# Second expert mixture: outputs copied aside before they are added, and the block's steps in another order

## The chip, the cores and the metric

The kernel runs on one core of one Trainium2 chip. The metric is device time in microseconds (us): 885.04 us before the change, the median of three runs (881.98 to 886.37). A profiled execution gives the trace; its span is 889.0 us.

## The reference

Two transformer layers over 2048 tokens of width 256 (2 batches of 1024), with a context of 154 rows per batch. Each layer is a cross attention and then a mixture of experts; both have a residual, and a layer norm ahead of them. The change lies in the mixture of the second layer:

```
logits = x @ Wg.T                      # 8 experts
top_v, top_i = top_k(logits, 2)        # two experts per token
gates = softmax(top_v)
# each expert takes at most 640 tokens
h = einsum('ecd,edf->ecf', exp_batches, W1)   # width 2 x 512
inp, gate = split(h, 2)
h = gelu(inp, exact) * gate
exp_out = einsum('eci,eid->ecd', h, W2)       # back to 256
out = segment_sum(gate_of_token * exp_out, token)
```

## The kernel before, in words

Both mixtures work in the same way, with the same functions and a layer object `l` (`l.n` is 0 or 1, `l.r` its prefix for semaphores, "r0" or "r1"). The normalised rows of the tokens are scattered by expert into a DRAM tensor `rows`, each row as two float16 parts (high and low) and four numbers at its end: the token, the second gate, the gain and the first expert. A table on the chip says at which block each expert begins. A block is 256 rows; where the last block of an expert holds at most 128 rows, TensorE computes only 128 of them. The second mixture has 19 blocks: experts of 3, 3, 1, 3, 1, 3, 3 and 2 blocks, of which 13 are whole and 6 are half blocks, each the last of its expert.

All products are made of float16 parts: high times high, high times low, low times high. In the second mixture the hidden width is 512, four chunks of 128 or two pairs of chunks (`pairs` is 2). One block g goes through the engines like this:

- ScalarE's queue loads the rows of a block into `x_raw` (L1253, `load`, two blocks ahead). TensorE turns them (L933, `turn_block`, one block ahead, after the gate and up products of block g), and VectorE copies the turned rows from PSUM into `xbT` (L1783) and works out each row's token and gate into `carried` (L1786 to L1790); this is `turned`. `x_raw` may be loaded again when `carried` is written.
- TensorE makes gate and up products (L685, output to `ps`) of pair 0 and pair 1, 48 matmuls. ScalarE applies Gelu (L1267), VectorE multiplies with the up product (L1804, into `h32`), ScalarE casts to float16 (L1271, `h_hi`), VectorE takes the difference (L1809, `h_lo`).
- TensorE makes the down products (L685, 24 matmuls in a whole block, 12 in a half one): in a first pass all high chunks, in a second all low chunks. It waits for the output of block g-1 to have left PSUM (semaphore `_y`).
- ScalarE scales the outputs into `yb` (L1280, two instructions). It waits for the down products and until the addition of block g-1 has landed (semaphore `_added`), since there is one `yb`.
- GpSimd (POOL) copies the token numbers of the block into `row_to` (L571), waits for `yb`, and issues two indirect DMAs that add 128 rows each to the output in DRAM (L575). It waits until both have landed (`_stored`), signals `_added` (L580), and only then goes on to the next block. Between experts it also loads the next two entries of the table (L567, L568).

The weights of an expert come in three chunks of 128x1024 float32. In the first block of each of the experts 0 to 5 the chunks of the expert two further on are split: ScalarE casts the high part (L1129, `high_part`), VectorE subtracts the low part (L1405). `l.beside` and `l.low_beside` say after which step of the block which chunk comes. Each engine works through its own program in order; nothing but these semaphores sets the order between engines. POOL's program is the loop `add_results`, called by `rest_of_experts`.

Of the kernel before, what the change touches and what calls it, by code (L numbers as in the profile page):

```python
# [22 lines left out]
P = 128  # L23
# [5 lines left out]
E = 8  # L29
# [42 lines left out]
def two_layers(nc, a, out):  # L72
    with ExitStack() as ctx:
# [183 lines left out]
        blk_passed = sb("blk_passed", [P, AHEAD, E], BF16)  # L257
        row_to = sb("row_to", [P, 2], I32)
        slot_s = sb("slot_s", [P, NT, TOP], I32)
        cnt = sb("cnt", [P, E])  # L260
# [231 lines left out]
        def _(pool):  # L492
# [71 lines left out]
            def add_results(l, e):  # L564
# [4 lines left out]
                with pool.Fori(first, end) as g:  # L569
# [10 lines left out]
                    pool.sem_inc(S(r + "_added"), 1)  # L580

            def scale_phi():

# [15 lines left out]
            def rest_of_experts(l):  # L599
                pool.wait_ge(S(l.r + "_kept"), 16 * NG)  # L600
                pool.wait_ge(S(l.r + "_table"), 1)
                with pool.Fori(0, E - 1) as e:
                    add_results(l, e)
                add_results(l, E - 1)

# [77 lines left out]
        def _(pe):  # L683
# [240 lines left out]
            def experts(l):  # L924
# [12 lines left out]
                def one_block(g, wh, wl, width):  # L937
# [15 lines left out]
                    turn_block(g + 1)  # L953
                    pe.wait_ge(S(r + "_y"), g + 1)
                    for c in range(l.hc):
                        if c % 2 == 0:
# [152 lines left out]
        def _(act):  # L1109
# [133 lines left out]
            def experts(l):  # L1243
# [11 lines left out]
                def one_block(g, coming=None):  # L1255

                    def split(step):
                        if coming:
                            for n in l.beside[step]:
                                high_part(l, *coming, n)  # L1260

                    for j in range(pairs + 1):
                        n = g * pairs + j
# [11 lines left out]
                    load(g + 2)  # L1275
                    split(pairs)
                    act.wait_ge(S(r + "_down"), g + 2)
                    wait_counted(act, S(r + "_added"), g + 1)
                    for hf in range(2):
# [22 lines left out]
                act.wait_ge(S(r + "_xbT_ps"), 2)  # L1302
                act.wait_ge(S(r + "_carried"), 1)
                load(1)
# [72 lines left out]
        def _(dve):  # L1377
# [397 lines left out]
            def experts(l):  # L1775
# [5 lines left out]
                def turned(g):  # L1781
# [8 lines left out]
                    dve.tensor_tensor(own[:, :, 0], share[:, :], raw[:, :, SECOND], ALU.add).then_inc(S(r + "_carried"), 1)  # L1790

                raw = x_raw[:, :, :].bitcast(F32)
                def low_part(e, slot, n):
                    low_part_of(l, e, slot, n)

                def one_block(g, coming=None):

                    for j in range(pairs + 1):
                        n = g * pairs + j
# [36 lines left out]
                else:  # L1836
                    coming_low_parts(1)
                turned(0)
                with dve.Fori(0, E // l.slots - 1) as pr:
# [136 lines left out]
```

## Time and profile before

| | |
|---|---|
| median of 3 runs | 885.04 us (881.98 to 886.37) |
| span of the profiled execution | 889.0 us |
| busy in the span: PE, DVE, ACT, POOL | 700.3, 547.8, 403.1, 302.8 us |
| second mixture, first to last block on PE | 711 to 872 us of the span |
| PE busy from 711 to 880 us | 144.60 of 169.00 us |

The span is the time from the first to the last instruction of the profiled execution, which was a little longer than the three timed runs. Times in the rows are microseconds from the start of the span. In a row of the timeline the bracket gives how long the engine had been idle before it and what ended that.

### The profile page before, as it was taken

What the parts mean: (1) busy time and instruction counts of PE and PEld (TensorE: products, weight loads), DVE (VectorE), ACT (ScalarE), POOL (GpSimd) and SP (SyncE); (2) the same over time, 40 slices, a digit from 0 to 9 for tenths busy, and PEclk for the clock granted to TensorE, in tenths of its full rate; (3) what the DMA queues carried; (4) which work ended last, traced back from release to release, by engine and by line L of the source; (5) the groups of instructions that cost most, each with busy time, mean ns of one, the idle gap of its engine ahead of it and who ended that gap; (6) DMA issues with size and microseconds to landing.
All of it is one profiled execution on the core that took longest, in us unless ns stands there. A gap on an engine that the chain in (4) does not pass through costs nothing.

```text
span 889.0 us, 19049 instructions
## 1 busy us (share of the span) xinstructions
PE 700.3 (79%) x6278; PEld 550.1 (62%) x6278; DVE 547.8 (62%) x1322; ACT 403.1 (45%) x720; POOL 302.8 (34%) x306
## 2 busy tenths in 40 slices
PE   5476796989564799999999899996862098898981
PEld 4232454555354688888897798895531087777771
DVE  7768576887836545647556656547696446566441
ACT  1135466576513434646545555442552044546331
POOL 7505301416337422222121131232167414334342
PEclk9689799989776799999999999997875599999996
DMA  4562300601524542536344643425022555464332
GB/s 140 118 141 51 59 2 24 180 24 49 153 81 151 185 129 36 165 51 171 78 126 98 170 112 101 107 39 179 25 101 95 174 170 131 115 147 114 63 55 40
DMA packets 68418, 92.24 MB, mean 104 GB/s; under 512 B 14442, under 2 KB 54435, under 8 KB 68348
## 3 DMA queue, kind: packets, MB, share of 16 engines
q1 hardware_dynamic: 41788, 63.37, 24.1%
q0 software_dynamic: 14592, 16.24, 10.6%
q10 hardware_dynamic: 11968, 11.72, 5.3%
q8 instruction: 42, 0.69, 0.3%
q14 instruction: 28, 0.23, 0.1%
HBM read 64.21 MB, written 29.87 MB: 106 GB/s over the span
## 4 chain that ended last, share of the span: by engine, by line
PE 48%; DVE 18%; issue 11%; ACT 9%; POOL 5%; DMA 5%; ACTq 2%; another core or an unknown queue 1%; DVEq 0%; POOLq 0%; SPq 0%
PE ps L685 45%; POOL rows L631 3%; DVE probs L1726 3%; DVE mx L1591 2%; DMA out_x<-keys,row_to 2%; DVE keys L1804 2%; DMA probs<-rows 2%; ACT probs L1189 1%; ACT probs L1271 1%; ACT expo L1186 1%; DVE keys L1783 1%; ACT probs L1267 1%; PE ps L933 1%; DVE stats L1383 1%; ACTq L1252 1%
## 5 line engine op out<-in xcount | busy, mean ns | idle before, releaser
L1804 DVE TENSOR_TENSOR keys<-probs,ps 128x512 f32<-128x512 f32 x122 | 82.8, 687 | 177.3 <-ACT probs L1267 86.3
L685 PE MATMUL ps<-keys,slot 128*128 128x256 f16 (+1 forms) x1440 | 146.5, 263 | 5.4 <-DVE keys L1783 2.7
L685 PE MATMUL ps<-keys,probs 128*128 128x256 f16 (+1 forms) x1488 | 139.5, 255 | 5.1 <-DVE probs L1405 3.7
L685 PEld LDWEIGHTS ps<-keys,slot 128*128 128x128 f16 x1440 | 127.8, 99 | 22.8 <-issue 5.4
L685 PEld LDWEIGHTS ps<-keys,probs 128*128 128x128 f16 x1488 | 124.2, 98 | 19.0 <-issue 7.2
L575 POOL DMA_INDIRECT attended<-keys,row_to x42 | 67.2, 1601 | 166.0 <-ACT keys L1280 142.2
L1267 ACT ACTIVATE probs<-ps 128x512 f32<-128x512 f32 x122 | 71.4, 598 | 65.9 <-PE ps L685 63.7
L1280 ACT ACTIVATE keys<-ps,carried 128x256 f32<-128x256 f32 x80 | 33.5, 470 | 117.9 <-POOLq L580 41.6
L1809 DVE TENSOR_TENSOR probs<-keys,probs 128x512 f16<-128x512 f32 x122 | 83.3, 688 | 3.6 <-ACT probs L1271 1.9
L1271 ACT CAST probs<-keys 128x512 f16<-128x512 f32 x122 | 74.8, 614 | 22.0 <-DVE keys L1804 21.9
L1726 DVE TENSOR_TENSOR probs<-expo,probs 128x512 f16<-128x512 f32 x80 | 61.1, 775 | 34.1 <-ACT probs L1189 28.2
L685 PE MATMUL ps<-slot,probs 128*128 128x256 f16 x636 | 74.8, 273 | 3.7 <-ACT probs L1271 3.0
L685 PE MATMUL ps<-probs 128*128 128x256 f16 x612 | 72.4, 273 | 4.8 <-ACT probs L1271 4.4
L575 POOL DMA_INDIRECT out_x<-keys,row_to x38 | 58.8, 1548 | 45.6 <-ACT keys L1280 36.6
L1186 ACT ACTIVATE expo<-ps 128x512 f32<-128x512 f32 x80 | 48.2, 602 | 52.8 <-PE ps L685 46.9
L685 PEld LDWEIGHTS ps<-slot,probs 128*128 128x128 f16 x636 | 60.0, 98 | 14.4 <-ACT probs L1271 4.2
L685 PEld LDWEIGHTS ps<-probs 128*128 128x128 f16 x612 | 57.5, 98 | 15.8 <-ACT probs L1271 4.5
L571 POOL COPY row_to<-carried 128x2 int32 x40 | 10.1, 252 | 139.0 <-issue 45.5
L933 PE MATMUL ps<-identh,probs 128*128 128x128 f16 x336 | 26.5, 224 | 36.5 <-DMA probs<-rows 36.5
L685 PE MATMUL ps<-penalties,identb 128*128 128x462 bf16 x96 | 34.8, 363 | 22.2 <-DVE queries L1569 9.4
L1189 ACT CAST probs<-expo 128x512 f16<-128x512 f32 x80 | 49.0, 619 | 0.0
L1405 DVE TENSOR_TENSOR probs<-inbox,probs 128x1024 f16<-128x1024 f32 x36 | 43.6, 1221 | 6.1 <-ACT probs L1129 6.0
(285 smaller groups left out, 1145.7 us busy)
## 6 DMA issues: line engine op xcount, KB each, us to landing
inbox<-in_W SPq DMA_DIRECT2D x24, 512.0 KB, 3.9
probs<-rows ACTq DMA_DIRECT2D x44, 260.0 KB
inbox<-in_wg SPq DMA_DIRECT2D x16, 512.0 KB, 5.2
inbox<-in_wu SPq DMA_DIRECT2D x16, 512.0 KB, 3.7
inbox<-in_wd SPq DMA_DIRECT2D x16, 512.0 KB, 4.2
rows<-zeros SPq DMA_DIRECT2D x16, 260.0 KB
x<-in_x SPq DMA_DIRECT2D x4, 512.0 KB, 6.1
q_out<-queries SPq DMA_DIRECT2D x8, 256.0 KB, 2.1
```

Source lines behind the costliest of these rows:

```text
L575: pool.indirect_dma_start(out=l.sums, out_offset=bass.IndirectOffsetOnAxis(ap=row_to[:, hf:hf + 1], axis=0), in_=yb[:, hf, :], in_offset=N ...
L685: return pe.matmul(o, l, r, start=start, stop=stop, **kw)
L933: last = pe.transpose(psh[:, 6, part * BLK + hf * P:part * BLK + (hf + 1) * P], x_raw[:, hf, part * P:(part + 1) * P], identh[:, :])
L1186: act.activation(e_ring[:, u % 4, :], ps[:, 4 + u % 2, :], ACT.Exp, scale=float(DK) ** -0.5).then_inc(S("a0_exp"), 1)
L1189: act.copy(p_hi[:, u - 1, :], e_ring[:, (u - 1) % 4, :]).then_inc(S("a0_phi"), 1)
L1267: act.activation(s_act[:, j % 2, :], ps[:, 2 * (j % 2), :], l.act).then_inc(S(r + "_s"), 1)
L1271: act.copy(h_hi[:, 2 * j - 2:2 * j, :].rearrange("p c t -> p (c t)"), h32[:, (j - 1) % 2, :]).then_inc(S(r + "_hh"), 1)
L1280: ins = act.activation(yb[:, hf, :], ps[:, 4 + hf, 0:D], ACT.Identity, scale=carried[:, bass.ds(g, 1), hf, 0:1].rearrange("p b d -> p (b d)"))
L1405: dve.tensor_tensor(w[:, 1, at:at + CH], stage[:, n % STAGES, :], w[:, 0, at:at + CH], ALU.subtract).then_inc(S(f"w_ready{l.n}"), 1)
L1726: dve.tensor_tensor(p_lo[:, u, :], e_ring[:, u % 4, :], p_hi[:, u, :], ALU.subtract).then_inc(S("a0_plo"), 1)
L1804: dve.tensor_tensor(h32[:, j % 2, :], s_act[:, j % 2, :], ps[:, 2 * (j % 2) + 1, :], ALU.mult).then_inc(S(r + "_h32"), 1)
L1809: dve.tensor_tensor(h_lo[:, 2 * j - 2:2 * j, :].rearrange("p c t -> p (c t)"), h32[:, (j - 1) % 2, :], h_hi[:, 2 * j - 2:2 * j, :].rearran ...
```

## The change

All of it is for the second mixture (`l.n` is 1); the first keeps its code.

- GpSimd copies `yb` into a new tensor `y_sent` (128x512 float32) after it has waited for `yb`, and the two indirect DMAs read from `y_sent`. A new semaphore `_taken` says that the copy is made. ScalarE's outputs wait for `_taken` of block g-1 and no longer for `_added`.
- TensorE's down products go pair by pair: high and low chunks of pair 0, then of pair 1, 24 matmuls as before.
- `turned` is cut in two. `turned_rows` copies the turned rows into `xbT` and the four numbers of each row into a new small tensor `tail_now` (128x8), which frees `x_raw` (semaphore `_raw_free`); it stands ahead of the difference of the last pair. `own_shares` works out `carried` from `tail_now`, after that difference.
- ScalarE's order in a block is Gelu, cast, Gelu, cast, where it was Gelu, Gelu, cast, cast. VectorE's is product, difference, product, (turned rows), difference.
- Of the three weight chunks ScalarE casts the first after the load and ahead of the outputs, the two others after the outputs; VectorE takes all three differences at the end of the block.

The core of the diff:

```
+        y_sent, _ = part(keys, 0, [P, 2, D])
-            l.beside = (([0], [1], [2], [3, 4], [5]), ([0], [1, 2], []))[n]
-            l.low_beside = (([0], [1], [2], [3], [4, 5]), ([0], [], [1, 2]))[n]
+            l.beside = (([0], [1], [2], [3, 4], [5]), ([], [0], [1, 2]))[n]
+            l.low_beside = (([0], [1], [2], [3], [4, 5]), ([], [], [0, 1, 2]))[n]
+            def copy_and_add_results(l, e):
...
+                with pool.Fori(first, end) as g:
+                    wait_counted(pool, S(r + "_carried"), g + 1)
+                    pool.tensor_copy(row_to[:, :], carried[:, bass.ds(g, 1), :, 1].bitcast(I32).rearrange("p b h -> p (b h)")).then_inc(S(r + "_to"), 1)
+                    wait_counted(pool, S(r + "_to"), g + 1)
+                    wait_counted(pool, S(r + "_y"), g + 2)
+                    pool.tensor_copy(y_sent[:, :, :], yb[:, :, :]).then_inc(S(r + "_taken"), 1)
+                    wait_counted(pool, S(r + "_taken"), g + 2)
+                    for hf in range(2):
+                        pool.indirect_dma_start(
+                            out=l.sums, out_offset=bass.IndirectOffsetOnAxis(ap=row_to[:, hf:hf + 1], axis=0),
+                            in_=y_sent[:, hf, :], in_offset=None, bounds_check=N - 1, oob_is_err=False,
+                            compute_op=ALU.add).then_inc(S(r + "_stored"), 16)
+                    pool.wait_ge(S(r + "_stored"), g * 32 + 32)
+                    pool.sem_inc(S(r + "_added"), 1)
...
+                def outputs_by_pairs(g, wh, wl, width):
+                    for j in range(pairs):
+                        pe.wait_ge(S(r + "_hh"), g * pairs + j + 1)
...
+                                mm(o, h_hi[:, c, tk], wh[:, at:at + D], c == 0, False)
+                                mm(o, h_hi[:, c, tk], wl[:, at:at + D], False, False)
+                        pe.wait_ge(S(r + "_h"), g * pairs + j + 3)
...
+                                last = mm(o, h_lo[:, c, tk], wh[:, at:at + D], False, c == l.hc - 1)
...
+                        act.wait_ge(S(r + "_xbT_ps"), g + 3)
+                        act.wait_ge(S(r + "_raw_free"), g + 2)
+                        load(g + 2)
+                        split(pairs - 1)
+                        results(g)
+                        split(pairs)
...
+                def results(g):
                     act.wait_ge(S(r + "_down"), g + 2)
-                    wait_counted(act, S(r + "_added"), g + 1)
+                    wait_counted(act, S(r + ("_taken" if l.n else "_added")), g + 1)
...
+                def turned_rows(g):
+                    dve.wait_ge(S(r + "_xbT_ps"), g + 2)
+                    dve.tensor_copy(xbT[:, :, :, :].rearrange("p a b c -> p (a b c)"), psh[:, 6, :]).then_inc(S(r + "_xbT"), 1)
+                    wait_counted(dve, S(r + "_share"), g + 1)
+                    dve.tensor_copy(tail_now[:, :, :], raw[:, :, TOKEN:TOKEN + 4].bitcast(I32)).then_inc(S(r + "_raw_free"), 1)
```

On POOL, the loop over the blocks of the last expert of the second mixture; `yb` and `y_sent` both lie in the arena `keys`. Before:

```order
L571 ISA [waits r1_carried]
L571 COPY row_to<-carried 128x2
L322 REGISTER_ALU [waits r1_to]
L575 DMA out_x<-keys,row_to 2048x256 [waits r1_y]
L575 DMA out_x<-keys,row_to 2048x256
L579 ISA
L569 REGISTER_ALU [waits r1_stored]
L569 COMPARE_AND_BRANCH
```

The same loop after the change:

```order
L591 ISA [waits r1_carried]
L591 COPY row_to<-carried 128x2
L324 REGISTER_ALU [waits r1_to]
L594 COPY keys<-keys 128x512 [waits r1_y]
L597 DMA out_x<-keys,row_to 2048x256 [waits r1_taken]
L597 DMA out_x<-keys,row_to 2048x256
L601 ISA
L589 REGISTER_ALU [waits r1_stored]
L589 COMPARE_AND_BRANCH
```

One copy stands between the wait for `_y` and the first DMA, and the DMA now waits for that copy; the wait for `_stored` at the end of the turn is where it was.

On ACT, the end of the first block of an expert, where the weights of a later expert are cast (`probs<-inbox`) and the outputs are written (`keys<-ps,carried`). Before:

```order
L1129 CAST probs<-inbox 128x1024 [waits staged_0]
L1270 REGISTER_ALU
L1271 CAST probs<-keys 128x512 [waits r1_h32]
L1129 CAST probs<-inbox 128x1024 [waits staged_1]
L1129 CAST probs<-inbox 128x1024 [waits staged_2]
...
L1253 DMA probs<-rows 128x2x260
L322 REGISTER_ALU [waits r1_down]
L1280 ISA [waits r1_added]
L1280 ACTIVATE keys<-ps,carried 128x256
L1280 ISA
L1280 ACTIVATE keys<-ps,carried 128x256
```

After the change:

```order
L1317 CAST probs<-keys 128x512 [waits r1_h32]
...
L1301 DMA probs<-rows 128x2x260
L1177 CAST probs<-inbox 128x1024 [waits staged_0]
L324 REGISTER_ALU [waits r1_down]
L1348 ISA [waits r1_taken]
L1348 ACTIVATE keys<-ps,carried 128x256
L1348 ISA
L1348 ACTIVATE keys<-ps,carried 128x256
L1177 CAST probs<-inbox 128x1024 [waits staged_1]
L1177 CAST probs<-inbox 128x1024 [waits staged_2]
```

The load of rows is issued ahead of all three weight casts; one cast stands ahead of the outputs and two behind them, and the outputs wait for `_taken`.

## Rows read from the trace of the kernel before

**Rows 1.** The page: the span, and the last difference of a pair on DVE.
```profile
span 889.0 us, 19049 instructions
...
L1809 DVE TENSOR_TENSOR probs<-keys,probs 128x512 f16<-128x512 f32 x122 | 83.3, 688 | 3.6 <-ACT probs L1271 1.9
```

**Rows 2.** Busy time by engine in the second mixture: start:end, length, busy (instructions).
```profile
711.00:880.00 169.00, 144.60 (x1448) 121.07 (x1448) 89.19 (x173) 76.88 (x133) 63.98 (x57) 0.97 0.50 110
```

**Rows 3.** Waits between 705 and 889 us: who for whom, total, times, longest.
```profile
ACT keys L1280 <- POOLq L580: 41.6, 11, 4.4
```

**Rows 4.** PE's timeline: start, length, line, idle before. Two whole blocks around a half.
```profile
746.99 5.41 PE L685 MATMUL ps<-keys,slot 128*128 128x256 f16 x48
...
755.59 2.84 PE L685 MATMUL ps<-keys,slot 128*128 128x128 f16 x48
...
762.13 5.41 PE L685 MATMUL ps<-keys,probs 128*128 128x256 f16 x48 [0.28 <-DVE keys L1783]
```

**Rows 5.** POOL's timeline: first and last addition, and first and last handover within an expert.
```profile
725.76 1.60 POOL L575 DMA_INDIRECT out_x<-keys,row_to  x1 [13.88 <-ACT keys L1280]
...
732.20 0.19 POOL L571 COPY row_to<-carried 128x2 int32 x1 [2.96 <-DMA out_x<-keys,row_to]
...
875.11 0.19 POOL L571 COPY row_to<-carried 128x2 int32 x1 [2.96 <-DMA out_x<-keys,row_to]
876.43 1.55 POOL L575 DMA_INDIRECT out_x<-keys,row_to  x1 [1.14 <-ACT keys L1280]
878.29 1.54 POOL L575 DMA_INDIRECT out_x<-keys,row_to  x1 [0.30 <-issue]
```

**Rows 6.** POOL's timeline: the seven handovers at an expert's begin, with one's DMAs.
```profile
748.18 0.38 POOL L571 COPY row_to<-carried 128x2 int32 x1 [3.30 <-DVE carried L1790]
...
774.57 0.19 POOL L571 COPY row_to<-carried 128x2 int32 x1 [4.74 <-issue]
775.80 1.55 POOL L575 DMA_INDIRECT out_x<-keys,row_to  x1 [1.04 <-issue]
777.66 1.54 POOL L575 DMA_INDIRECT out_x<-keys,row_to  x1 [0.30 <-issue]
782.94 0.21 POOL L571 COPY row_to<-carried 128x2 int32 x1 [3.74 <-DVE carried L1790]
...
807.93 0.54 POOL L571 COPY row_to<-carried 128x2 int32 x1 [3.28 <-DVE carried L1790]
...
818.22 1.24 POOL L571 COPY row_to<-carried 128x2 int32 x1 [4.32 <-issue]
...
843.80 0.19 POOL L571 COPY row_to<-carried 128x2 int32 x1 [3.89 <-issue]
...
867.14 0.19 POOL L571 COPY row_to<-carried 128x2 int32 x1 [3.02 <-issue]
```

**Rows 7.** Costliest groups on POOL, by shape: a cast of 128 and a memset of 512.
```profile
L511 POOL MEMSET slot<- 128x512 f32 x1 | 0.5, 515 | 0.0
...
L502 POOL CAST identb<-ident 128x128 bf16<-128x128 f32 x1 | 0.3, 291 | 0.1
```

**Rows 8.** One line of POOL, float32 in, 256 wide: shortest/median/longest in ns.
```profile
L650 POOL CAST penalties<-xln x8: 397/398/498, 197.6 to 270.8; 128x256 f16<-128x256 f32 x8
```

**Rows 9.** ACT's timeline: the end of the first block.
```profile
719.66 1.99 ACT L1129 CAST probs<-inbox 128x1024 f16<-128x1024 f32 x2
723.36 0.38 ACTq L1253 DMA_DIRECT2D probs<-rows  x1
724.03 0.84 ACT L1280 ACTIVATE keys<-ps,carried 128x256 f32<-128x256 f32 x2 [2.38 <-issue]
```

**Rows 10.** DVE's timeline: low parts of weights at the end of a block.
```profile
817.06 2.35 DVE L1405 TENSOR_TENSOR probs<-inbox,probs 128x1024 f16<-128x1024 f32 x2
```

**Rows 11.** PE's timeline: the last down products of the first block.
```profile
721.50 0.61 PE L685 MATMUL ps<-slot,probs 128*128 128x256 f16 x4 [0.20 <-DVE probs L1809]
```

**Rows 12.** One line of POOL, 256 wide, once beside a DVE difference: shortest/median/longest.
```profile
L527 POOL CAST heads<-heads x3: 399/688/1488, 88.3 to 92.9; 128x256 bf16<-128x256 f32 x3
```

More of the change, by code:

```diff
@@ L258, in two_layers @@
         row_to = sb("row_to", [P, 2], I32)
+        tail_now = sb("tail_now", [P, 2, 4], I32)
         slot_s = sb("slot_s", [P, NT, TOP], I32)
@@ L580, in add_results @@
                     pool.sem_inc(S(r + "_added"), 1)
+            def copy_and_add_results(l, e):
+                tb, r = table[l.n], l.r
+                first = pool.value_load(tb[0:1, bass.ds(e, 1)], min_val=0, max_val=MAXBLK - 1)
+                end = pool.value_load(tb[0:1, bass.ds(e + 1, 1)], min_val=1, max_val=MAXBLK)
+                with pool.Fori(first, end) as g:
[12 more added lines that the diff above has]
+                    pool.sem_inc(S(r + "_added"), 1)
             def scale_phi():
@@ L601, in rest_of_experts @@
                 pool.wait_ge(S(l.r + "_table"), 1)
+                add = add_results if l.n == 0 else copy_and_add_results
+                if l.n:
+                    pool.sem_inc(S(l.r + "_taken"), 1)
                 with pool.Fori(0, E - 1) as e:
-                    add_results(l, e)
-                add_results(l, E - 1)
+                    add(l, e)
+                add(l, E - 1)
             def power(c, t0, n):
@@ L1260, in split @@
                                 high_part(l, *coming, n)
+                    if l.n:
+                        for j in range(pairs):
+                            n = g * pairs + j
+                            act.wait_ge(S(r + "_h32"), n + 1)
+                            act.wait_ge(S(r + "_gu_ps"), n * 2 + 1)
+                            act.activation(s_act[:, j % 2, :], ps[:, 2 * (j % 2), :], l.act).then_inc(S(r + "_s"), 1)
+                            act.wait_ge(S(r + "_h32"), n + 3)
+                            act.copy(h_hi[:, 2 * j:2 * j + 2, :].rearrange("p c t -> p (c t)"), h32[:, j % 2, :]).then_inc(S(r + "_hh"), 1)
+                            if j < pairs - 1:
+                                split(j)
+                        act.wait_ge(S(r + "_xbT_ps"), g + 3)
[4 more added lines that the diff above has]
+                        split(pairs)
+                        return
                     for j in range(pairs + 1):
@@ L1796, in one_block @@
                 def one_block(g, coming=None):
+                    if l.n:
+                        for j in range(pairs):
+                            n = g * pairs + j
+                            dve.wait_ge(S(r + "_s"), n + 1)
+                            dve.wait_ge(S(r + "_gu_ps"), n * 2 + 2)
+                            dve.wait_ge(S(r + "_h"), n + 1)
+                            dve.tensor_tensor(h32[:, j % 2, :], s_act[:, j % 2, :], ps[:, 2 * (j % 2) + 1, :], ALU.mult).then_inc(S(r + "_h32"), 1)
+                            if j == 0:
+                                dve.wait_ge(S(r + "_down"), g + 1)
+                            if j == pairs - 1:
+                                turned_rows(g + 1)
+                            dve.wait_ge(S(r + "_hh"), n + 1)
+                            dve.tensor_tensor(h_lo[:, 2 * j:2 * j + 2, :].rearrange("p c t -> p (c t)"), h32[:, j % 2, :],
+                                              h_hi[:, 2 * j:2 * j + 2, :].rearrange("p c t -> p (c t)"), ALU.subtract).then_inc(S(r + "_h"), 1)
+                        own_shares(g + 1)
+                        if coming:
+                            for c in l.low_beside[pairs]:
+                                low_part(*coming, c)
+                        return
                     for j in range(pairs + 1):
```

32 lines of the change are left out of this document (30 added, 2 removed).

## The prediction

> **What bounds the kernel now.** I read the page first, then the busy times by stretch, then the waits and the timelines of the second mixture, engine by engine. The change touches only that mixture, some 169 us of a span of 889.0 us, in which PE is busy for 144.60 us [rows 1, 2]. So PE has little idle time to give back there, and the question is who makes it idle. The waits name POOL: ScalarE's outputs waited 41.6 us in 11 cases for the signal that an addition has landed [rows 3]. PE's timeline shows what that does: a whole block with nothing in its way takes 8.60 us (746.99 to 755.59), a half block 6.54 us (755.59 to 762.13), although its matmuls are only half as many [rows 4]. All 13 whole and 6 half blocks at these paces would be 151.0 us.
>
> Next to this stands POOL's own loop, which decides my forecast. Its 19 turns run from the first addition at 725.76 to the last at 876.43 us, 18 intervals in 150.67 us, 8.37 us each [rows 5]. A turn has parts that it can't avoid: from the end of the second DMA issue to the next `row_to` copy (the landing and the loop) 2.94 us on average over the 11 handovers within an expert (the first and the last are 2.96) [rows 5]; the copy itself 0.19; 1.04 from the copy to the DMA where nothing is waited for; two issues of 1.55 and 1.54 with 0.30 between them, 3.39 [rows 6]. That is 7.56 us. At the seven handovers to a new expert, where POOL also loads table entries, the idle time ahead of the copy is 3.30, 4.74, 3.74, 3.28, 4.32, 3.89 and 3.02 us, 3.76 on average, so the turn has 8.38 us; and four of these copies took 0.38, 0.21, 0.54 and 1.24 us, together 1.6 us more than 0.19 each [rows 6]. The sum of what POOL can't avoid is 11 x 7.56 + 7 x 8.38 + 1.6 = 143.4 us. POOL therefore has only 150.67 - 143.4 = 7.3 us to spare in the whole mixture. Before, it is nearly as much the bound as PE.
>
> **The change part by part.** *The copy on POOL.* Each turn gets a copy of 128x512 float32 and one more counted wait, behind the landing of the block before and ahead of its own DMAs, so all of it lies on POOL's loop. No row shows this copy. From below: a memset of that shape, which reads nothing, took 0.515 us [rows 7]. The casts read float32 at 291 ns for 128 elements [rows 7] and 398 ns for 256 [rows 8], 0.84 ns per further element; carried on to 512 that is 0.61 us, and I take this. The added wait: from the end of a `row_to` copy to the DMA there were 1.04 us with two waits already met [rows 6], and from the end of ScalarE's output (724.03 + 0.84) to the DMA at 725.76 us 0.89 us with one [rows 5, 9]; so a wait costs about 0.15. A turn grows by 0.76 us, 18 of them by 13.7 us.
>
> *The copy beside VectorE.* At 818.22 us a `row_to` copy took 1.24 us, and it ended at 819.46, just when a pair of weight differences that began at 817.06 and lasted 2.35 us had ended at 819.41 [rows 6, 10]. A POOL copy that meets such a difference waits for its end. The differences of a block take 2 x 0.688 us [rows 1], and in six of 19 blocks three weight differences of some 1.2 us come on top, 1.16 us per block: 2.5 us in 8.4, a chance of 0.3, and half a difference to wait (0.46 us), 0.14 us per turn or 2.5 us in all. The Trainium skill, page "SBUF — State Buffer", section "Who interferes with whom", states this as a lock: a VectorE instruction with two SBUF inputs and a GpSimd instruction that reads SBUF block each other, the second to come waiting until the first has finished. By this rule the 2.5 us belong in the sum, and the rows agree; without it the forecast would be 2.5 us lower. The lock would also hold VectorE back by up to a copy's length, which costs nothing as long as PE isn't the bound.
>
> *ScalarE waits for the copy.* The wait that goes (41.6 us) doesn't free POOL: its DMAs are issued, and their landing waited for, in the same order and number. What it gives is one block more of lead for PE. PE uses it up: its first 18 blocks at the paces of rows 4 need 144.5 us, POOL's 18 turns now need 143.4 + 13.7 + 2.5 = 159.6. Whatever lead PE gets, it ends by waiting for `_y` again, that is for POOL's copy. The stall moves from ScalarE's wait for `_added` to ScalarE's and PE's waits for `_taken` and `_y`.
>
> *The first output.* Before, ScalarE cast two weight chunks until 721.65 us, issued a load at 723.36 and wrote the first output at 724.03, although PE's down products had ended at 722.11 [rows 9, 11]. With the load earlier and two casts behind the output it may begin at about 722.3, 1.7 us earlier; the first copy takes 0.76 of it back. The first addition starts 1.0 us earlier.
>
> *The rest.* Down products by pairs are the same 24 matmuls with other waits; Gelu and cast in turn make the chain of a half block longer by about a cast and a difference (1.3 us at most), and the earlier output gives some of it back; the tail copy (128x8) adds one short instruction to VectorE per block; the earlier free `x_raw` starts loads earlier. The cast that now stands ahead of the outputs waits for its staged chunk, and the output, PE's next down products and POOL's copy are queued behind it; the two casts behind the outputs delay the next block's first Gelu, and all three differences the next product. I cost all of this at nothing either way: the 15 us by which PE is ahead of POOL over the mixture cover it. If that cover is gone it would be up to 1.3 us in each half block, 8 us, or the same gained from the loads.
>
> **The sum.** 13.7 + 2.5 - 7.3 (POOL's spare time, used up) - 1.0 = +7.9 us. What follows the last issue (878.29 + 1.54 to 889.0, 9.2 us) stays [rows 1, 5]. So the profiled span goes from 889.0 to about 897 us; it is 4 us over the median of the runs shown, and the same difference on that median, 885.04, gives 892.9 us, 0.9% slower.
>
> **The rivals.** *PE sets the end (faster).* If POOL's turns shrink by themselves, for instance because landings and table loads at an expert's begin (3.02 to 4.74 us) are as short as those within (2.94), that takes 7 x 0.8 + 1.6 = 7 us off its loop; with the copy at its lower end (9.3 us) POOL would need 146 us and PE's 151.0 us would decide, from about 161 us now (its first to last block, 711 to 872 us): at most 10 us less; I take 7, 878 us. For it speaks the wait of 41.6 us; against it, that the cases with 4.74 and 3.89 us waited for nothing shown, thus are POOL's own time. It decides from the point where a turn with its copy is below PE's 7.9 us on average. Chance 0.12.
>
> *No change.* The copy costs its lower bound, 0.515 us, and the wait nothing: 9.3 - 7.3 - 1.2 = +0.8, 886 us. For it speaks that the price of 0.61 us is carried on from casts of half the size; against it, that a memset doesn't read. Chance 0.22.
>
> *The copy is slow.* A cast of 256 elements on POOL took 1.488 us where others took 399 ns [rows 12]; a copy of 512 hit like that takes 1.70 us, a turn 1.85 more, 33 us in all, or +25 us; if half of the copies are hit, +16 us, 901 us. For it speaks that the weight differences now come together, close to the time of the outputs. Chance 0.08.
>
> **How the numbers follow.** The forecast, POOL's loop longer by its copy, has 0.58; its own range is 888 to 899 us (a turn longer by 0.5 to 1.1 us, the rest of the sum as it stands). 0.5% of 885.04 is 4.4 us, about what a measurement of this kernel tells from no change. Faster (below 880.6): the first rival, 0.12. Same (to 889.5): the second and a small part of the forecast's own range, 0.25. Slower: 0.63. The range of 884 to 903 us leaves out the first rival and the worst of the third.
>
> **What would show it.** Right: POOL's additions 8.4 to 9.3 us apart from the third block on, nearly all with "issue" ahead of them and no wait for ScalarE; the new copy at 0.6 us, longer where VectorE subtracts; PE idle ahead of its down products, waiting for `keys` outputs; last addition at about 884 us of the span. Wrong: POOL waiting for ScalarE before most copies, or additions 8.0 us apart or closer; PE's blocks at 8.6 and 6 us without idle time to the end.

## The result, and the profile after

The changed kernel takes 904.95 us (median of 4 runs, 900.27 to 908.31) beside 884.08 us of the kernel before on the same chip: ratio 1.0225, 95% interval 1.0195 to 1.0256. The forecast was 892.9 us with a range of 884 to 903: slower, as forecast, but by 21 us where 8 were worked out.

On the page of the changed kernel, the span, the group of POOL's additions (busy, mean ns of one, idle before) and the weights' loads by SP (median us from issue to landing):

```profile
span 902.0 us, 19115 instructions
...
L597 POOL DMA_INDIRECT out_x<-keys,row_to x38 | 62.6, 1648 | 22.5 <-POOL keys L594 16.8
...
inbox<-in_W SPq DMA_DIRECT2D x24, 512.0 KB, 5.3
```

The mean issue is 1648 ns, where it was 1.55 and 1.54 us [rows 6], and no idle time of POOL's DMAs is put down mainly to ScalarE any more.

Busy time by engine in the second mixture (start:end, length, then PE, PE weight loads, DVE, ACT, POOL, granted clock, DMA share, GB/s):

```profile
704.60:890.00 185.40, 150.21 (x1448) 124.19 (x1448) 93.49 (x192) 77.49 (x133) 77.47 (x75) 0.92 0.44 100
```

Against [rows 2] the stretch is 16 us longer with the same 1448 matmuls; PE stands idle for 35 us where it did for 24. PE's busy time grew by 5.6 us; the granted clock, a mean between its two levels of 1.2 and 2.4 GHz, is 0.92 of the upper one, where it was 0.97, in a stretch in which PE stands idle longer. The mixture now begins at 704.65 us, in the profile before at 711.12; the two profiled runs differ by 6 us before the change's code begins, so that the spans differ by 13 and the medians by 21. I therefore compare the time from the first to the last addition.

POOL's timeline, the first two DMAs, a turn with nothing in its way, and the last two (start, length, idle before):

```profile
717.63 1.79 POOL L597 DMA_INDIRECT out_x<-keys,row_to  x1 [0.89 <-POOL keys L594]
719.72 1.58 POOL L597 DMA_INDIRECT out_x<-keys,row_to  x1 [0.30 <-issue]
...
797.72 0.19 POOL L591 COPY row_to<-carried 128x2 int32 x1 [2.86 <-DMA out_x<-keys,row_to]
798.24 0.61 POOL L594 COPY keys<-keys 128x512 f32<-128x512 f32 x1 [0.33 <-POOL row_to L591]
799.73 1.56 POOL L597 DMA_INDIRECT out_x<-keys,row_to  x1 [0.88 <-POOL keys L594]
801.59 1.54 POOL L597 DMA_INDIRECT out_x<-keys,row_to  x1 [0.30 <-issue]
...
889.42 1.56 POOL L597 DMA_INDIRECT out_x<-keys,row_to  x1 [0.88 <-POOL keys L594]
891.29 1.54 POOL L597 DMA_INDIRECT out_x<-keys,row_to  x1 [0.30 <-issue]
```

From 717.63 to 889.42 are 171.8 us in 18 turns, where [rows 5] have 150.7: 21.1 us more, about the whole of the loss. In a free turn `row_to` ends at 797.91 and the DMA begins at 799.73: 1.82 us (0.33 + 0.61 + 0.88), where it was 1.04. All 18 turns show this 1.82 within 0.03 us, so POOL waits for no output after the first.

But the turns at a new expert look otherwise. POOL's timeline there:

```profile
775.08 0.44 POOL L591 COPY row_to<-carried 128x2 int32 x1 [5.57 <-issue]
...
777.36 2.37 POOL L597 DMA_INDIRECT out_x<-keys,row_to  x1 [0.88 <-POOL keys L594]
780.04 2.48 POOL L597 DMA_INDIRECT out_x<-keys,row_to  x1 [0.31 <-issue]
789.44 0.18 POOL L591 COPY row_to<-carried 128x2 int32 x1 [6.92 <-issue]
...
818.37 1.04 POOL L591 COPY row_to<-carried 128x2 int32 x1 [6.53 <-issue]
```

DVE's weight differences at that time, SP's weight loads there, and two pieces of the chain of waits (start, length, what):

```profile
777.07 1.23 DVE L1473 TENSOR_TENSOR slot<-inbox,slot 128x1024 f16<-128x1024 f32 x1 [1.07 <-ACT slot L1177]
778.74 2.36 DVE L1473 TENSOR_TENSOR slot<-inbox,slot 128x1024 f16<-128x1024 f32 x2 [0.45 <-ACT slot L1177]
...
818.14 1.23 DVE L1473 TENSOR_TENSOR probs<-inbox,probs 128x1024 f16<-128x1024 f32 x1 [1.07 <-ACT probs L1177]
```

```profile
778.47 3.13 SPq L425 DMA_DIRECT2D inbox<-in_W  x3
```

```profile
780.04 7.26 DMA out_x<-keys,row_to
...
801.59 3.78 DMA out_x<-keys,row_to
```

The handovers of 5.57, 6.92 and 6.53 us answer to 4.74, 3.74 and 4.32 in [rows 6]. Two things happen at 777 to 790 us. The two issues take 2.37 and 2.48 us instead of 1.55, and beside them VectorE subtracts weights from 777.07 to 778.30 and from 778.74 to 781.10. And the second addition lands 7.26 us after its issue began, against 3.78 us for one with no loads beside it; three weight chunks of 512 KB were issued from 778.47 on within 3.13 us.

POOL's 18 turns, cut into their parts (sums from POOL's timeline of each run; us). The columns: the 11 handovers within an expert, the 7 at a new expert, the 36 issues, the `row_to` copies, and the time from `row_to` to the first DMA; with the 0.30 between two issues 18 times, they make the time from the first to the last addition.

| | first to last | within | new expert | issues | `row_to` | to the DMA |
|---|---|---|---|---|---|---|
| before | 150.7 | 32.3 | 26.3 | 55.7 | 5.0 | 25.9 |
| after | 171.8 | 35.4 | 33.2 | 59.5 | 5.4 | 32.9 |
| more | 21.1 | 3.1 | 6.9 | 3.8 | 0.4 | 7.0 |

The last column is the forecast's own term: 18 x 0.78 = 14.0 us of copy and wait, less the 7 us that POOL had waited. The other 14 us were not in it.

### The profile page after: what moved, and what is told of

Read it like the earlier page. It is cut to its first block, busy times and chain, and to the rows that moved or that the text cites. A ratio compares the mean times of both kernels' runs of the same rounds, so it can differ in the third digit from the quotient of the medians.

```text
span 902.0 us, 19115 instructions
## 1 busy us (share of the span) xinstructions
PE 706.6 (78%) x6266; PEld 556.6 (62%) x6278; DVE 552.0 (61%) x1342; ACT 403.7 (45%) x720; POOL 318.9 (35%) x325
## 4 chain that ended last, share of the span: by engine, by line
PE 43%; DVE 16%; issue 13%; DMA 10%; POOL 7%; ACT 7%; POOLq 2%; ACTq 1%; DVEq 0%; SPq 0%
PE ps L710 40%; DMA out_x<-keys,row_to 7%; POOL rows L656 3%; DVE probs L1794 3%; DVE mx L1659 2%; ACT probs L1237 1%; POOL keys L594 1%; ACT expo L1234 1%; PE ps L958 1%; POOL out_x L597 1%; DVE stats L1451 1%; DVE keys L1907 1%; DMA probs<-rows 1%; POOL row_to L591 1%; DVE probs L1912 1%
## 5 line engine op out<-in xcount | busy, mean ns | idle before, releaser
L710 PE MATMUL ps<-keys,slot 128*128 128x256 f16 (+1 forms) x1440 | 149.2, 266 | 4.8 <-DVE keys L1907 2.5
L710 PE MATMUL ps<-keys,probs 128*128 128x256 f16 (+1 forms) x1488 | 141.9, 257 | 4.7 <-DVE probs L1473 3.8
L1794 DVE TENSOR_TENSOR probs<-expo,probs 128x512 f16<-128x512 f32 x80 | 61.0, 774 | 33.4 <-ACT probs L1237 33.2
L1332 ACT ACTIVATE probs<-ps 128x512 f32<-128x512 f32 x84 | 50.0, 597 | 53.1 <-PE ps L710 52.7
L597 POOL DMA_INDIRECT out_x<-keys,row_to x38 | 62.6, 1648 | 22.5 <-POOL keys L594 16.8
L1912 DVE TENSOR_TENSOR probs<-keys,probs 128x512 f16<-128x512 f32 x84 | 57.6, 685 | 1.5 <-ACT probs L1336 0.3
L1336 ACT CAST probs<-keys 128x512 f16<-128x512 f32 x84 | 51.5, 613 | 12.2 <-DVE keys L1907 12.1
```

Of the source, the lines that this page charges most:

```text
L597: pool.indirect_dma_start(out=l.sums, out_offset=bass.IndirectOffsetOnAxis(ap=row_to[:, hf:hf + 1], axis=0), in_=y_sent[:, hf, :], in_offs ...
L710: return pe.matmul(o, l, r, start=start, stop=stop, **kw)
L1332: act.activation(s_act[:, j % 2, :], ps[:, 2 * (j % 2), :], l.act).then_inc(S(r + "_s"), 1)
L1336: act.copy(h_hi[:, 2 * j - 2:2 * j, :].rearrange("p c t -> p (c t)"), h32[:, (j - 1) % 2, :]).then_inc(S(r + "_hh"), 1)
L1794: dve.tensor_tensor(p_lo[:, u, :], e_ring[:, u % 4, :], p_hi[:, u, :], ALU.subtract).then_inc(S("a0_plo"), 1)
L1912: dve.tensor_tensor(h_lo[:, 2 * j - 2:2 * j, :].rearrange("p c t -> p (c t)"), h32[:, (j - 1) % 2, :], h_hi[:, 2 * j - 2:2 * j, :].rearran ...
```

## The experiments

The question is where the other 14 us come from. They may come from the moved weight casts and the loads that follow them; from the copy, which makes POOL late; or from the new order of products, Gelu and casts. And what lengthens issues and landings may be the weight loads in the DMA engines, or VectorE's subtractions beside POOL, or both. Every kernel was timed in 3 or 5 rounds beside the kernel before. The letters in the expectations are explained where they stand, D and L under the small loads; the text below goes by what each theory says. The times are medians of several runs, the time from the first to the last addition comes from one profiled execution of each kernel, so that the two can differ by some microseconds.

**The copy alone** (kernel before, with POOL's copy and ScalarE's wait for `_taken`; all else as before).

```
-                    wait_counted(act, S(r + "_added"), g + 1)
+                    wait_counted(act, S(r + ("_taken" if l.n else "_added")), g + 1)
...
+                    pool.tensor_copy(y_sent[:, :, :], yb[:, :, :]).then_inc(S(r + "_taken"), 1)
+                    wait_counted(pool, S(r + "_taken"), g + 2)
```

> The kernel before with nothing but the copy to y_sent, the additions from it, and ScalarE's outputs waiting for the copy. Theory A (the copy lengthens POOL's loop by 0.78 us a turn, and the additions land late only because the weight casts were moved, which makes three weight loads start together beside them): 18 x 0.78 = 14.0, less the 7.3 us that POOL had to spare, +7 us, 891 us, landings as before. Theory B (a loop that is always late meets the weight loads wherever the casts stand): about +18 to +20 us, 903 us, with landings of 6 to 8 us as in the changed kernel.

Measured 901.06 us, ratio 1.0179 (1.0149 to 1.0208); first to last addition 164.4 us, 14 more than before. Of the two times expected, 891 us (the copy costs its own term and the moved casts the rest) and 903 us, the second is the nearer one: the moved casts are not needed for a loss of about 16 us (1.8%). POOL's timeline at one of its two late handovers, and SP's loads there:

```profile
766.34 2.35 POOL L596 DMA_INDIRECT out_x<-keys,row_to  x1 [0.88 <-POOL keys L593]
768.99 1.54 POOL L596 DMA_INDIRECT out_x<-keys,row_to  x1 [0.30 <-issue]
777.05 1.04 POOL L590 COPY row_to<-carried 128x2 int32 x1 [6.52 <-issue]
```

```profile
764.55 4.32 SPq L424 DMA_DIRECT2D inbox<-in_W  x3
```

The pair is issued in the middle of the loads. In the kernel before the loads of this place are issued between two pairs; SP's timeline there:

```profile
770.76 4.32 SPq L423 DMA_DIRECT2D inbox<-in_W  x3
```

The last of the three is issued by 775.08 us, and the next pair at 775.80 [rows 6]. So with the casts at their old place, too, the copy costs more than its own 7 us.

**The change without the copy** (ScalarE waits for `_added` again).

```
-                add = add_results if l.n == 0 else copy_and_add_results
+                add = add_results
...
-                    wait_counted(act, S(r + ("_taken" if l.n else "_added")), g + 1)
+                    wait_counted(act, S(r + "_added"), g + 1)
```

> The changed kernel without the copy: additions from yb, ScalarE's outputs wait for the landing again; all else (pairs, early turned rows, moved casts) stays. Theory A: the 13.7 us of longer landings and issues stay in part, less POOL's 7.3 us to spare, about +4 to +7 us, 890 us. Theory B: without the copy the loop isn't late, about the time before, 884 us. Theory C (ScalarE's new order Gelu, cast, Gelu, cast makes PE's blocks longer, and that is the loss): close to the changed kernel, 900 us or more, with PE idle inside its down products and POOL waiting for ScalarE.

896.49 us, 1.0113 (1.0081 to 1.0144): between the 890 us expected of the moved casts and the 900 us expected of the new order. **The casts and differences back** in the changed kernel:

```
-            l.beside = (([0], [1], [2], [3, 4], [5]), ([], [0], [1, 2]))[n]
-            l.low_beside = (([0], [1], [2], [3], [4, 5]), ([], [], [0, 1, 2]))[n]
+            l.beside = (([0], [1], [2], [3, 4], [5]), ([0], [1, 2], []))[n]
+            l.low_beside = (([0], [1], [2], [3], [4, 5]), ([0], [], [1, 2]))[n]
...
-                            if j < pairs - 1:
-                                split(j)
+                            split(j)
...
+                            if coming:
+                                for c in l.low_beside[j]:
+                                    low_part(*coming, c)
```

> The changed kernel with the weight casts and differences where they stood before (first chunk after the first pair's cast and difference, the two others after the second pair's cast and at the end of the block); the copy and all else stay. Theory A: the longer landings and issues (13.7 us) go, 905 - 13 = 892 us, additions about 8.8 us apart. Theory B: no gain, 902 to 905 us. Theory C: no gain, 902 to 905 us.

897.63 us, 1.0149 (1.0119 to 1.0178): again between the times expected, 892 us and 902 or more. **The casts moved, alone**, in the kernel before (the same two lines the other way, and the casts behind the outputs):

```
-                    split(pairs)
+                    split(pairs if l.n == 0 else pairs - 1)
...
+                    if l.n:
+                        split(pairs)
```

> The kernel before with nothing but the weight casts and differences moved as in the change (first cast ahead of the outputs, two behind them, three differences at the block's end). Theory A: some of the 13.7 us of longer landings and issues appear, less the 7.3 us to spare, +4 to +7 us, 890 us. Theory B and theory C: no change, 884 us.

899.5 us, 1.0162 (1.0132 to 1.0192), more than any theory gave it (890 us at most). First to last addition of the three: 165.7, 165.1 and 166.6 us. So between the additions the copy alone costs 14 us and the moved casts alone 16, and together they cost 21 (by the times about 16, 14 and 20): they don't add. None of the theories A, B and C covers these four runs. In the change without the copy a turn has no copy in it, and POOL's timeline still has a handover of 7.45 us, at a place where SP issues three loads:

```profile
746.45 2.01 POOL L577 DMA_INDIRECT out_x<-keys,row_to  x1 [0.30 <-issue]
755.91 0.19 POOL L573 COPY row_to<-carried 128x2 int32 x1 [7.45 <-DMA out_x<-keys,row_to]
757.23 1.55 POOL L577 DMA_INDIRECT out_x<-keys,row_to  x1 [1.14 <-ACT keys L1346]
```

```profile
744.41 3.13 SPq L425 DMA_DIRECT2D inbox<-in_W  x3
```

**The order alone** (the change without the copy and with the casts back: pairs, Gelu and cast in turn, rows turned early).

> The changed kernel without the copy and with the weight casts where they stood before: what is left is the pairs one by one, Gelu and cast in turn, and the rows turned ahead of the last difference. Theory D: POOL is late where it was before, so no landing grows, 884 us, within 4 us. If the order by itself moves additions onto the loads: 890 us or more.

884.52 us (10 runs), 0.9995 (0.9977 to 1.0013); 151.3 us. The order costs and gains nothing within 2 us, so the new order of Gelu and casts is not the loss.

**Small loads** (of the weights of the last six experts of the second mixture only 64 of 1024 columns of a chunk are loaded; the rest of each weight is missing), in the changed kernel and in the one before.

```
+                few = CH // 16 if l.n and not isinstance(e, int) else CH
-                sp.dma_start(stage[:, n % STAGES, :], w[:, col:col + CH]).then_inc(S(f"staged_{n}"), 16)
+                sp.dma_start(stage[:, n % STAGES, 0:few], w[:, col:col + few]).then_inc(S(f"staged_{n}"), 16)
```

> The changed kernel, but the weight loads of the second mixture's experts 2 to 7 bring only 64 of 1024 columns of each chunk (so the outputs of these experts are not the reference's); number, order and waits of all instructions stay. Theory D (an addition that is under way when three weight loads start lands only when these have landed, because they share the DMA engines): handovers fall to 2.9 us within an expert and about 3.5 at a new one, the first to the last addition take about 159 us and the time is 892 us. Theory L (VectorE's weight differences, with two inputs in SBUF, hold up POOL's making of descriptors and its table loads; the loads have no part): no change, 903 to 906 us, landings of 6 to 8 us stay.

> The kernel before with the same small weight loads (outputs of experts 2 to 7 of the second mixture are not the reference's). Theory D: little is held up by the loads before the change, since additions start behind two of three loads: 0 to 5 us less, 881 to 885 us. If it gains more than 8 us, the loads cost the kernel before too, by another way than the additions.

The changed kernel falls to 895.0 us (1.0115, 1.0082 to 1.0147), 164.5 us; the kernel before stays at 883.57 (0.9992, 0.9972 to 1.0012). So full loads cost the kernel before nothing and the changed one some 10 us, 7.3 of them between the additions. Of the times expected for the changed kernel, 892 us if additions wait for the loads is nearer than 903 if the loads have no part, but it isn't reached. In POOL's timeline the handovers shrink, the issues do not:

```profile
800.50 2.07 POOL L598 DMA_INDIRECT out_x<-keys,row_to  x1 [0.88 <-POOL keys L595]
802.87 2.54 POOL L598 DMA_INDIRECT out_x<-keys,row_to  x1 [0.31 <-issue]
808.69 0.21 POOL L592 COPY row_to<-carried 128x2 int32 x1 [3.28 <-issue]
```

**Small differences** (full loads; VectorE subtracts only 32 of the 1024 columns for these experts).

```
-                dve.tensor_tensor(w[:, 1, at:at + CH], stage[:, n % STAGES, :], w[:, 0, at:at + CH], ALU.subtract).then_inc(S(f"w_ready{l.n}"), 1)
+                few = 32 if l.n and not (isinstance(e, int) and e < 2) else CH
+                dve.tensor_tensor(w[:, 1, at:at + few], stage[:, n % STAGES, 0:few], w[:, 0, at:at + few], ALU.subtract).then_inc(S(f"w_ready{l.n}"), 1)
```

> The changed kernel, but VectorE's weight differences of the experts 2 to 7 in the second mixture take 32 of 1024 columns (their low parts are not the reference's); the loads are whole. Theory D: landings of 6 to 8 us stay beside the loads, 900 to 905 us; only the DMA issues that had grown (1.55 to 2.4 us) fall back, 3 to 4 us at most. Theory L: landings fall to 3.8 us, 892 us.

906.04 us, 1.0232 (1.0196 to 1.0267), 174.0 us, at the upper end of the 900 to 905 us expected if landings beside the loads stay long. Now the issues are short and the landings long; POOL's timeline at the same place:

```profile
776.63 1.56 POOL L597 DMA_INDIRECT out_x<-keys,row_to  x1 [0.88 <-POOL keys L594]
778.50 1.54 POOL L597 DMA_INDIRECT out_x<-keys,row_to  x1 [0.30 <-issue]
787.87 0.19 POOL L591 COPY row_to<-carried 128x2 int32 x1 [7.82 <-issue]
```

In the chain of waits the second of these additions lands 7.22 us after its issue began, although the issue itself is as short as ever (from the start of the issue, then SP's loads there):

```profile
778.50 7.22 DMA out_x<-keys,row_to
```

```profile
775.37 4.04 SPq L425 DMA_DIRECT2D inbox<-in_W  x3
```

The two runs separate the two mechanisms. The differences make the issues long: 59.5 us in the changed kernel, 55.9 with small differences. The loads make the landings long: all 18 handovers take 68.6 us in the changed kernel and 60.6 with small loads. Neither is the whole. Beside full loads the differences cost no time of their own: when they go, the landings take as much.

**The copy alone with small loads.**

> The kernel before with GpSimd's copy and the outputs that wait for the copy alone; and of the weights of the last six experts of the second mixture only 64 of 1024 columns of each chunk are loaded (the rest is what lay there before). With full loads the copy alone gave 901 us, 17 us over the kernel before; a copy and its wait of 0.76 us in 18 turns less 7.3 us to spare explain 7 us of them. If the other 10 us come from additions that meet the weight loads: handovers at a new expert back to about 27 us in seven (30.75 with full loads), within an expert about 32 in eleven, first to last addition 156 to 159 us, about 892 us. If the copy alone costs more by itself (GpSimd and VectorE at one time, or the copy's own turn): first to last addition 162 us or more, 898 us or more.

896.11 us, 1.0135 (1.0112 to 1.0158), 163.1 us: between the two cases and nearer to the second one, against the theory that the loads are all that the copy meets. The handovers at a new expert fell to 25.1 us, but the issues grew to 60.9. Then **both small**, in the changed kernel (e14 in the second expectation) and with the copy alone:

> The changed kernel; of the weights of the last six experts of the second mixture only 64 of 1024 columns of each chunk are loaded and only 32 subtracted on VectorE. If loads and differences together make up what lies above the copy's own term: issues 55.7 us (3.10 a pair), handovers at a new expert about 26 us and within an expert about 32, between the additions 33, first to last addition 156 to 159 us, 889 to 892 us. If something else than these two makes GpSimd's turns longer: 162 us or more, 895 us or more.

> The kernel before with the copy alone, and weights' loads and differences small as in e14. If loads and differences together make up what lies above the copy's own term: issues 55.7 us, first to last addition 156 to 158 us, 890 to 892 us (before 884, copy and wait 14 us less the 7 that were to spare). If the copy costs more by itself: still 896 us.

890.32 us (10 runs; 1.0063, 1.0042 to 1.0084) and 890.88 us (7 runs; 1.0067, 1.0040 to 1.0094); first to last addition 158.3 and 157.3 us, 7.6 and 6.6 more than before. The same place in POOL's timeline of the changed kernel with both small:

```profile
775.83 1.56 POOL L598 DMA_INDIRECT out_x<-keys,row_to  x1 [0.88 <-POOL keys L595]
777.70 1.54 POOL L598 DMA_INDIRECT out_x<-keys,row_to  x1 [0.31 <-issue]
782.98 0.18 POOL L592 COPY row_to<-carried 128x2 int32 x1 [3.74 <-issue]
```

Its second addition lands after 3.13 us, with an issue as long as in the run with small differences alone, where it took 7.22:

```profile
777.70 3.13 DMA out_x<-keys,row_to
```

This closes the account of the sums: with small loads and differences the change costs 7.6 us between the additions and about 6 us in the time, which is the copy's own term of 7 us; the copy costs nothing further by itself. The two are not additive (171.8 us with both, 164.5 without the loads, 174.0 without the differences, 158.3 without either): the differences cost nothing beside full loads and 6.2 us beside small ones. A likely reason is that an addition that no longer meets the one comes at another moment and meets the other; it was not followed from place to place.

**One loop for the additions** (POOL adds all 19 blocks in one loop, without table loads between experts), in the kernel before, in the order alone, in the changed kernel, and in the changed kernel with the casts back.

```
-                first = pool.value_load(tb[0:1, bass.ds(e, 1)], min_val=0, max_val=MAXBLK - 1)
-                end = pool.value_load(tb[0:1, bass.ds(e + 1, 1)], min_val=1, max_val=MAXBLK)
+                first = 0 if e is None else pool.value_load(tb[0:1, bass.ds(e, 1)], min_val=0, max_val=MAXBLK - 1)
+                end = pool.value_load(tb[0:1, 8:9] if e is None else tb[0:1, bass.ds(e + 1, 1)], min_val=1, max_val=MAXBLK)
```

> The kernel before, but GpSimd adds all 19 blocks of the second mixture in one loop instead of one loop for each expert, so that no table entries are loaded between experts. If GpSimd's turns with their table loads set the pace of the kernel before nearly as much as the products do (7.3 us to spare, worked out from the handovers): the seven handovers at a new expert fall from 26.3 us to about 20.6 (2.94 each), first to last addition 146 to 149 us, 879 to 882 us, 0.2 to 0.5% faster. If the products alone set the pace: the handovers fall, ScalarE's waits for the addition fall too, and the time stays at 884 us within 1 us.

> The order of the change (products by pairs, Gelu and cast in turn, rows turned early) without the copy and with the weight casts where they were before, which gave 884.5 us and a first to last addition of 151.3 us; now GpSimd adds all 19 blocks of the second mixture in one loop, no table loads between experts. If GpSimd bounds this order: handovers at a new expert from 27.6 to about 21 us, first to last addition 145 to 148 us, 878 to 881 us. If the products bound it: 884 us within 1 us.

> The changed kernel, but GpSimd adds all 19 blocks of the second mixture in one loop, without table loads between experts. In the kernel before this took 10.8 us off the handovers and nothing off the time. If GpSimd's turns bound the changed kernel in all its blocks: what goes from the seven handovers (10 us, from 33 to about 23) comes off the time, 893 to 898 us. If the loads, met at another moment, or the products hold it: 901 us or more.

> The changed kernel with the weight casts and differences where they were before (897.6 us, first to last addition 165.1 us), and GpSimd's additions in one loop without table loads between experts. If GpSimd's turns are the bound: the handovers at a new expert from 31 to about 20 us, first to last addition about 154 us, 885 to 888 us; with the shorter turns the products may come to bound the end, and it can't get under about 880 us. If the loads decide: 893 us or more.

Kernel before: 884.46 us (12 runs; 1.0008, 0.9994 to 1.0023). Its handovers at a new expert fell from 26.3 to 15.5 us, and the time from `row_to` to the DMA rose from 25.9 to 37.3: what POOL saved it waited for outputs. Two rows of its timeline:

```profile
742.47 0.18 POOL L571 COPY row_to<-carried 128x2 int32 x1 [1.81 <-DMA out_x<-keys,row_to]
746.35 1.54 POOL L575 DMA_INDIRECT out_x<-keys,row_to  x1 [3.69 <-ACT keys L1283]
```

The order alone: 882.36 us (12 runs; 0.9988, 0.9969 to 1.0006), not to be told from the kernel before. The changed kernel: 897.84 us (1.0148, 1.0111 to 1.0186), 7 us less than 904.95 and within the 893 to 898 expected of POOL as the bound; its handovers at a new expert fell by 7.3 us, the time between the additions by 5.0. There POOL's own time is the bound, in the kernel before it is not. With the casts back: 893.9 us (1.0098, 1.0066 to 1.0131), where 885 to 888 were expected of POOL as the bound and 893 or more if the loads decide: the handovers at a new expert fell by 7.6 us, but the issues grew by 1.6, the handovers within an expert by 1.8 and `row_to` and what follows it up to the DMA by 1.4, so that only 2.8 us were left. That the additions came at other moments is the likely reason. No version here beats the kernel before by more than its interval.

## Why the prediction was right and where it was wrong

- **The copy and its wait: right.** 0.61 us was worked out and 0.61 measured; a turn grew by 0.78 where 0.76 was said. 18 turns make 14.0 us, against 13.7.
- **POOL's spare time, 7.3 us: right as a size.** The time from `row_to` to the DMA fell back to its floor in every turn, and with loads and differences small the change costs 6.6 to 7.6 us. The working behind it took the table loads for POOL's time without cover; in the kernel before they lay beside ScalarE's outputs (one loop gives nothing there) and become bare only once POOL is the bound (one loop gives 7 us in the time, 5 between the additions). Beside this, [rows 4] were misread: the half block has as many gate and up matmuls as the whole one, 48, each half as wide (2.84 us for 5.41); the paces of 8.60 and 6.54 us are as read, so no sum hangs on it.
- **Where the stall goes: right for ScalarE, half right for PE.** ScalarE's outputs now wait for POOL's copy, in the waits of the changed kernel (who for whom, total, times, longest), in place of [rows 3]:

```profile
ACT keys L1348 <- POOL keys L594: 29.6, 9, 6.3
...
PE ps L710 <- ACT probs L1317: 20.0, 21, 4.6
```

  No wait of PE for the outputs (`_y`) shows. PE waits for ScalarE's cast, and the longest of these waits, 4.63 us, ends with a cast that stands behind an output which waited 6.35 us for the copy (first PE's timeline, then ACT's). The sum of 20.0 us is not the copy's: in the change without the copy PE's waits for the cast make 20.8 us, none longer than 2.0.

```profile
793.80 1.44 PE L710 MATMUL ps<-probs 128*128 128x256 f16 x6 [4.63 <-ACT probs L1317]
...
790.79 0.84 ACT L1348 ACTIVATE keys<-ps,carried 128x256 f32<-128x256 f32 x2 [6.35 <-POOL keys L594]
791.52 0.60 ACT L1315 ACTIVATE probs<-ps 128x512 f32<-128x512 f32 x1
793.04 0.62 ACT L1317 CAST probs<-keys 128x512 f16<-128x512 f32 x1 [0.93 <-DVE keys L1888]
```

- **The signs named: in part.** POOL does wait for nobody's output after the first. But of the 16 intervals from the third addition on, ten are 8.2 to 8.7 us and six 9.2 to 14.1, where 8.4 to 9.3 was forecast for nearly all: the undisturbed turn came out as worked out, the disturbed ones were not in the forecast.
- **The first output: nearly.** The first addition comes 12.98 us after PE's start (717.63 - 704.65), before 14.64 (725.76 - 711.12): 1.7 us earlier, 1.0 was said.
- **The copy beside VectorE, 2.5 us: mis-placed.** Only the first copy took longer than 0.65 us, 0.82. What meets the differences is the issue: 3.8 us more in 36 of them, and they are short again when the differences are small. The Trainium skill, page "SBUF — State Buffer", section "Who interferes with whom", has a VectorE instruction with two SBUF inputs block a GpSimd instruction that reads SBUF. The `row_to` copy at 818.37 us agrees: it began beside the subtraction of 818.14, and both end at 819.4. The same section of the Trainium skill says that a `tensor_tensor` did not stall DMAs in a probe, and infers why descriptor making is free of it; the issue of 2.48 us here, 1.54 with small differences, speaks against carrying that to indirect DMAs.
- **The rest, "I cost all of this at nothing either way": this step failed.** It weighed the moved casts against PE's and ScalarE's cover, and asked what they delay on ScalarE and VectorE. But SP's `fetch` waits for the difference (`w_ready`) of a chunk before it loads the next one into the same buffer, so moving casts and differences moves three loads of 512 KB each, and POOL's own longer turn moves the additions against them. I had taken landing and issue as fixed (2.94, 3.76 and 1.55 us) from [rows 5, 6]. They rose by 3.1, 6.9 and 3.8 us in sum, 14 of the 21. It isn't the moved casts alone: the copy alone, with the casts at their old place, costs 14 us between the additions where this sum gives 7. That loads and differences together make these 14 us is shown by making both small, when 13.5 us go; that the landings are the loads' part is shown by 7.22 us with them and 3.13 without. The Trainium skill, page "DMA: Bandwidth & Descriptors", section "Queues, rings and completion order", says that each DMA engine takes turns between the queues that have work, packet by packet. These two landings agree with it.
- **The rivals.** PE as the bound and no change did not come. The slow copy came out at nearly the right time, 901 us, by a mechanism that was not there: the copies stayed at 0.61 us.

What stays open: the loss is shown for loads and differences together, not place by place, and its size depends on the moment at which each addition falls, which every edit here moved.

## What to carry to other kernels

When a step is moved, follow each buffer that it releases to the DMA that waits for the buffer, and lay that DMA's new time beside the transfers on the critical loop. A landing time read from the trace holds only as long as the other queues' traffic stays where it was; bound it from both sides like a cost that no row shows. When a loop becomes the bound, what was covered in it before (table loads, issues, late landings) begins to count, and the costs of the edits need not add.

## What the runs showed of the hardware

- An indirect DMA's issue on POOL took 1.55 us alone and up to 2.54 us beside a VectorE subtraction of 128x1024 float32, and 1.53 to 1.61 us in all 38 cases when these subtractions were 32 columns wide.
- From the start of its issue (1.54 us) a 128-row addition took 7.22 us to land where three 512 KB loads were issued from 3.1 us before it, and 3.13 us at the same place when these loads brought 1/16 of their columns.
- On POOL a float32 copy of 128x512 takes 0.61 us, and with the wait for its own end it adds 0.78 us to a turn (1.82 us from `row_to` to the DMA, 1.04 before).
